# Twelve unused fp16 matmuls ahead of a wait in a patch-embedding, scan and feed-forward kernel

## The chip, the cores and the metric

The kernel runs on one core of one Trainium2 chip. The metric is the device time of one execution in microseconds, the median over several runs. "Before" took 1426.93 us (three runs, 1425.58 to 1428.28).

## The reference

Images and text tokens go through three layers. The image `x` (32, 3, 224, 224) is cut into 14 by 14 patches of 16 by 16 pixels, each patch is layer-normalised, multiplied by a 768 by 256 matrix and normalised again; the 77 text tokens are appended, which makes 273 tokens of 256 features for each of the 32 images. Then comes a recurrent layer on every second token, and a gated feed-forward layer on all of them:

```python
h = tok_ref(x, W, bias, ln1_g, ln1_b, ln2_g, ln2_b)          # patches: layernorm, matmul, layernorm
h = concatenate([h, txt], axis=1)                            # 196 + 77 tokens
# attention layer: x_sub = rmsnorm(layernorm(h))[:, ::2]; x_proj, gate = split(x_sub @ w_in.T + b_in)
#   state = tanh(state * A + x_t * Bm);  y_t = state @ sum(Cm) + Dv * x_t     for each step t
#   out = (y * silu(gate)) @ w_out.T + b_out, each row repeated for two tokens
h = h + attn_ref(layernorm(h), w_in, b_in, A, Bm, Cm, Dv, w_out, b_out, g_norm)
h = h + ffn_ref(layernorm(h), w_gate, w_up, w_down)          # silu(gate) * up, then down
```

## The kernel before, in words

The 273 tokens are handled in 20 groups of 14 (the last has 7): groups 0 to 13 are one row of image patches each, 14 to 19 are text. The groups go through a pipeline, and iteration i of the program works on several of them at once: it normalises the pixels of group i+1 (the part called "ahead"), turns and embeds group i and projects it ("pre"), runs the recurrence of group i-1 ("scan"), finishes the recurrent layer and does the feed-forward layer of group i-2 up to its product ("post"), and does the down projection and the store of group i-3 ("down"). Iterations 0 to 2 fill the pipeline, iterations 3 to 12 are a loop with all parts, 13 is the last with image work, then come the text iterations and a tail.

Inside an iteration the order of work on each engine is written out by hand as 56 slots. Slot n holds step n of the scan: VectorE multiplies the state by A into one of four PSUM banks (`grow`, line 771), TensorE adds the input by one fp16 matmul (`drive`, line 1218), ScalarE takes the tanh (`squash`, line 976). Every eighth slot TensorE also reads out y with 16 matmuls (`read_step`, line 1228). All other parts are hung into slots by the table `PLANS` (lines 65 to 113). Each engine executes its list strictly in order, with semaphore waits in it.

What lies around the change, in image iterations, on TensorE:

- `shrink` (lines 1400 and 1401), the down projection of group i-3, in slots 1 to 7.
- `turn` (line 1273), eight groups of transposes of the normalised pixels of group i, in slots 7 to 14, into the banks P[0] and P[1] by turns. ScalarE copies each group out into `xT` (`xT_copy`, line 993), and counts `xT_done`. `turn(6)` is the last but one and the last in P[0]; its copy brings `xT_done` to g*8+7.
- `attend` (lines 1326 to 1341), slots 15 and 16: the output projection of the recurrent layer of group i-2. It waits for `z_done`, then for `xT_done` at g*8+7 (the bank P[0] is free), writes the bias into P[0] (line 1335), and adds the products of `zT` and `out_w` (line 1338).
- `embed` (line 1288), slots 17 to 28, `average` (line 1247), slots 19 and 21, `turn_fx` (line 1357), slot 32, the feed-forward matmuls `ffn` (lines 1385 and 1386), slots 34 to 52, `turn_xa` (line 1305) and `project` (line 1321), slots 35 to 48.

What `attend` waits for is a chain outside TensorE. After the last read-out ScalarE copies y out of PSUM (line 982), SyncE sends it to DRAM and back in another layout (lines 651 and 657), and GpSimd adds the skip term and multiplies by the gate (`gating`, lines 1121 and 1125), which counts `z_done`. Behind `attend` come the residual sum on VectorE (line 867), the normalisation and the feed-forward layer.

`fx_hi` is the fp16 part of the transposed, normalised activations, a tile of 128 by 2 by 448; ScalarE writes it at slot 31 (line 1050), and only `ffn` reads it. 

Of the kernel before, what the change touches and what calls it, by code (L numbers as in the profile page):

```python
# [37 lines left out]
KF = CH * PATCH * PATCH // 128  # L38
RAWP = CH * B
BIASP = 96  # L40
XA_AFTER, X_AFTER, GATE_AFTER = 1, 2, 4
X_SCALE, B_SCALE = 16.0, 64.0
U_SCALE = X_SCALE * B_SCALE
# [131 lines left out]
def build(nc, x, txt, W, tok_bias, ln1_g, ln1_b, ln2_g, ln2_b, w_in, b_in, A, Bm, Cm, Dv, w_out, b_out,  # L175
# [8 lines left out]
    with ctx:  # L184
        def sb(name, shape, dt=FP32):
            return ctx.enter_context(nc.sbuf_tensor(name, shape, dt))

        def sem(name):
            return ctx.enter_context(nc.semaphore(name))
# [18 lines left out]

        bias_one = sb("bias_one", [BIASP, PT], BF16)
        bias_row = sb("bias_row", [BIASP, D], BF16)  # L210
        h = sb("h", [128, RING, CW])
# [35 lines left out]
        fx_hi, fx_lo = (fx_split[:, n * DB * TOK:(n + 1) * DB * TOK].bitcast(FP16)  # L247
                        .rearrange("p (j t) -> p j t", j=DB) for n in range(2))
# [13 lines left out]
        P = [ctx.enter_context(nc.psum_tensor(f"P{n}", [128, 512], FP32)) for n in range(2)]  # L262
# [192 lines left out]
        def setup_tensor(pe):  # L455
            pe.wait_ge(s_w, 48)
            for f in range(KF):
                mm = pe.matmul(Y[0:PT, 0:D], b1[:, f:f + 1].to_broadcast([128, PT]), w_st[:, f, :],
                               start=(f == 0), stop=(f == KF - 1))
            mm.then_inc(s_bias, 1)  # L460
            pe.wait_ge(s_cst, 16)
            tensor_body(pe, -1, general=False, **AHEAD)
            pe.wait_ge(s_wts, 48)
            for n, (blocks, _, _) in enumerate(turns):
                if n == NU:
                    pe.wait_ge(s_row, 1)
                for k, src in enumerate(blocks):
                    mm = pe.transpose(turn_of(n)[:, k * 128:k * 128 + 128], src, ident)
                mm.then_inc(s_tr, 1)
# [83 lines left out]
        xT_done = sem("xT_done")  # L553
# [651 lines left out]
        def tensor_body(pe, i, image, ahead, pre, scan, post, down, steps, general):  # L1205
            r, g, s, q, d = i + 1, i, i - 1, i - 2, i - 3
# [102 lines left out]
            def project(part, k):  # L1309
# [13 lines left out]
                if k == DB - 1:  # L1323
                    mm.then_inc(proj_ps, 1)

            def attend(k):

                pe.wait_ge(z_done, q + 1)

                if pre and image:  # L1330
                    pe.wait_ge(xT_done, g * 8 + 7)
                elif down:
                    pe.wait_ge(out_done, d * 2 + 1)
                if k == 0:
                    pe.matmul(P[0][0:PT, 0:2 * D], bias_one[:, :], bias_row[:, :].unsqueeze(1).to_broadcast([BIASP, 2, D]),
                              start=True, stop=False, skip_group_check=True)
                for j in range(DB):
                    mm = pe.matmul(P[0][0:PT, k * D:k * D + D], zT[:, j, k * PT:k * PT + PT], out_w[:, j, :],
                                   start=False, stop=(j == DB - 1), skip_group_check=True)
                if k == 1:  # L1340
                    mm.then_inc(attn_ps, 1)
# [63 lines left out]
            for slot in range(SLOTS):  # L1405
# [22 lines left out]
                if post:  # L1428
                    for k in parts_at(plan, "attend", slot):
                        attend(k)  # L1430
# [55 lines left out]
        with nc.Block() as block:  # L1486
# [29 lines left out]
            @block.tensor  # L1516
            def _(pe):
                setup_tensor(pe)
                tensor_body(pe, 0, general=False, **HEAD[0])
                pe.wait_ge(s_bst, 1)  # L1520
                pe.wait_ge(s_read, 1)
                pe.wait_ge(s_brow, 9)
                pe.wait_ge(s_flag, 1)


                flag = pe.value_load(large_flag[:, :], min_val=0, max_val=1)
                with pe.If(flag > 0):
                    bodies(pe, tensor_body, general=True)
                with pe.Else():
                    bodies(pe, tensor_body, general=False)  # L1530
# [30 lines left out]
```

## Time and profile before

| | |
|---|---|
| median of three runs | 1426.93 us (1425.58 to 1428.28) |
| profiled execution | 1428.12 us |
| its span, first to last instruction | 1426.3 us |
| TensorE busy | 1224.9 us, 86% |
| VectorE busy | 1085.5 us, 76% |
| ScalarE busy | 1001.3 us, 70% |
| GpSimd busy | 434.4 us, 30% |
| mean granted TensorE clock | 0.943 of full speed |

The profiled execution's own time lies 1.8 us above its span, which is what stands around the first and the last instruction. Busy shares say which engine has most to do on average, and not what the end of an iteration waits for. The granted clock is the share of full speed that the throttle gave TensorE in a stretch: 1.00 is 2.4 GHz, 0.50 is 1.2 GHz, and a value between is a mixture of the two over the stretch.

### The profile page before, as it was taken

Reading aid. Unit: us, or ns where it says so; the run is one execution under the profiler, and the core shown is the slowest. Engines: PE = TensorE matmul, PEld = TensorE weight load, DVE = VectorE, ACT = ScalarE, POOL = GpSimd, SP = SyncE. Lnnn points to the kernel's source line nnn. Section 1 sums busy time; section 2 is a strip of 40 time slices with the busy share of each in tenths; the row PEclk is TensorE's granted clock in tenths of the full one; section 3 lists DMA queues with packets and bytes.
Section 4 is the critical chain, followed back from the end, with each engine's and each line's share of the span. In section 5 each row is a group of like instructions: output and inputs, shape, how many; then the busy total and the mean of one; then the engine's idle time right before and its main releaser. Section 6 shows DMA issues by size and latency. Waiting matters only on the chain.

```text
span 1426.3 us, 25870 instructions
## 1 busy us (share of the span) xinstructions
PE 1224.9 (86%) x7137; PEld 662.5 (46%) x7137; DVE 1085.5 (76%) x2412; ACT 1001.3 (70%) x1955; POOL 434.4 (30%) x437
## 2 busy tenths in 40 slices
PE   2658898989898989898989889899999999998976
PEld 2434445445454444454545445454444444434434
DVE  4549787778787878787778777877888888887833
ACT  2437686767777677768685858586888787787732
POOL 7404042424242423333232333331311321321220
PEclk8769899999999999999899989999999999999987
DMA  6230414140404050505040414130323222322210
GB/s 183 56 75 28 104 31 112 28 115 26 116 26 115 17 123 6 132 6 126 16 120 22 116 26 104 38 81 23 92 67 94 78 77 76 80 77 58 75 36 15
DMA packets 154671, 99.60 MB, mean 70 GB/s; under 512 B 129057, under 2 KB 143265, under 8 KB 153281
## 3 DMA queue, kind: packets, MB, share of 16 engines
q1 hardware_dynamic: 151120, 97.58, 26.9%
q10 hardware_dynamic: 3504, 1.46, 0.5%
q8 instruction: 23, 0.38, 0.1%
q14 instruction: 24, 0.19, 0.0%
HBM read 58.39 MB, written 40.60 MB: 69 GB/s over the span
## 4 chain that ended last, share of the span: by engine, by line
PE 36%; issue 22%; DMA 10%; ACT 9%; POOL 9%; DVE 8%; SPq 5%; POOLq 0%; DVEq 0%; ACTq 0%
PE Y L1228 6%; PE U L1218 6%; DMA y_scr<-y_fx 6%; PE P L1385 5%; PE P L1288 5%; PE P L1386 5%; DVE U L771 3%; PE P L1321 3%; DMA yT<-y_scr 3%; ACT h L976 3%; ACT rawn L987 2%; SPq L651 2%; DVE act L891 1%; POOL yT L1121 1%; POOL zT L1125 1%
## 5 line engine op out<-in xcount | busy, mean ns | idle before, releaser
L771 DVE TENSOR_TENSOR U<-h,a_col 128x512 f32<-128x512 f32 x1096 | 704.5, 689 | 147.7 <-ACT h L976 146.7
L976 ACT ACTIVATE h<-U 128x512 f32<-128x512 f32 x1096 | 608.1, 603 | 240.8 <-PE U L1218 239.1
L1218 PE MATMUL U<-x_diag,b_st 128*128 128x512 f16 x1096 | 370.2, 388 | 63.0 <-DVE U L771 45.1
L1228 PE MATMUL Y<-h,read_st 128*32 128x512 f32 x2192 | 271.0, 613 | 0.7 <-ACT h L976 0.7
L1218 PEld LDWEIGHTS U<-x_diag,b_st 128*128 128x128 f16 x1096 | 105.1, 100 | 220.8 <-DVE U L771 146.0
L1160 POOL TENSOR_TENSOR xT_act<-act,xT_act 128x448 f16<-128x448 f32 x114 | 117.5, 1040 | 195.1 <-ACT xT_act L1060 194.1
L1288 PE MATMUL P<-tok_w,xT_act 128*112 128x256 f32 x672 | 169.7, 391 | 2.3 <-ACT xT_act L993 2.3
L1288 PEld LDWEIGHTS P<-tok_w,xT_act 128*112 128x112 f32 x672 | 120.2, 182 | 54.0 <-issue 21.2
L1400 PE MATMUL P<-down_w,xT_act 128*112 128x256 bf16 x480 | 118.5, 282 | 6.9 <-POOL xT_act L1160 4.6
L1228 PEld LDWEIGHTS Y<-h,read_st 128*32 128x32 f32 x2192 | 58.2, 111 | 138.4 <-issue 114.9
L1401 PE MATMUL P<-down_w,xT_act 128*112 128x256 bf16 x480 | 117.4, 279 | 0.0
L891 DVE SCALAR_TENSOR_TENSOR act<-fsg,P 128x448 f32<-128x448 f32 x118 | 72.6, 615 | 52.5 <-PE P L1386 51.9
L1121 POOL TENSOR_TENSOR yT<-yT,gate_in 128x448 f32<-128x448 f32 x20 | 22.7, 1134 | 260.9 <-DMA yT<-y_scr 260.9
L993 ACT ACTIVATE xT_act<-P 128x384 f32<-128x384 f32 x112 | 83.2, 804 | 15.1 <-PE P L1273 13.2
L1385 PE MATMUL P<-fx_split,gate_w 128*128 128x448 f16 x228 | 81.7, 358 | 10.8 <-DVE fx_split L896 10.1
L1385 PE MATMUL P<-fx_split,up_w 128*128 128x448 f16 x236 | 86.4, 366 | 4.6 <-DVE act L891 4.6
L778 DVE BATCH_NORM_STATS2 raw_st<-raw 96x6 f32<-96x256 f32 x196 | 70.1, 410 | 24.8 <-DMA raw<-in_x 24.8
L1386 PE MATMUL P<-fx_split,up_w 128*128 128x448 f16 x236 | 86.3, 366 | 0.0
L1056 ACT ACTIVATE fsg<-P 128x448 f32<-128x448 f32 x114 | 62.4, 547 | 33.2 <-PE P L1386 30.4
L1386 PE MATMUL P<-fx_split,gate_w 128*128 128x448 f16 x228 | 81.8, 359 | 0.0
L1321 PE MATMUL P<-xaT,in_w 128*128 128x224 f32 x320 | 76.0, 369 | 6.0 <-ACT xf L1026 4.9
L1110 POOL TENSOR_TENSOR res_s<-res_s,half_th 112x4 f32<-112x4 f32 x20 | 20.6, 1028 | 189.8 <-DVE res_s L881 189.8
(152 smaller groups left out, 1517.3 us busy)
## 6 DMA issues: line engine op xcount, KB each, us to landing
raw<-in_x SPq DMA_DIRECT2D x42, 448.0 KB, 6.1
gate_scr<-gate_o SPq DMA_DIRECT2D x20, 448.0 KB, 2.5
gate_in<-gate_scr SPq DMA_DIRECT2D x20, 448.0 KB, 7.7
tok_scr<-tok SPq DMA_DIRECT2D x19, 448.0 KB, 3.3
res<-tok_scr SPq DMA_DIRECT2D x19, 448.0 KB, 3.7
out<-res SPq DMA_DIRECT2D x76, 112.0 KB, 2.3
x_diag<-scan_scr SPq DMA_DIRECT2D x312, 16.0 KB
x_diag<-scan_scr SPq DMA_DIRECT2D x304, 12.0 KB
```

Of the source, the lines that this page charges most:

```text
L771: dve.tensor_tensor(U[bank_of(slot)][:, :].rearrange("p (l b) -> p l b", b=B), h[:, (slot - CHUNKS) % RING, :].rearrange("p (l b) -> p l b ...
L891: dve.scalar_tensor_tensor(act[:, k, :], fsg[:, k % 2, :], ACT_SCALE * DEQUANT, up_bank(k, scan)[:, 0:4 * PT], ALU.mult, ALU.mult).then_in ...
L976: sc.activation(h[:, slot % RING, :], U[bank_of(slot)][:, :], ACT.Tanh, scale=1.0 / U_SCALE).then_inc(squashed, 1)
L1160: gp.tensor_tensor(act_lo[:, k, :], act[:, k, :], act_hi[:, k, :], ALU.subtract).then_inc(act_lo_done, 1)
L1218: pe.matmul(U[bank_of(slot)][:, :], b_st[:, c, :], x_diag[:, c, :, t * B:t * B + B], start=False, stop=True, skip_group_check=True).then_i ...
L1228: mm = pe.matmul(Y[c4 * 32:c4 * 32 + 32, :], read_st[:, t, half, :], h[:, (t * CHUNKS + half * RG + c4) % RING, :], start=(t == 0 and half ...
L1288: mm = pe.matmul(P[1 - k // 2][0:PT, (k % 2) * D:(k % 2) * D + D], xT[:, f, k // 2, (k % 2) * PT:(k % 2) * PT + PT], tok_w[:, f, :], start ...
L1321: mm = pe.matmul(P[1][:, k * TOK:k * TOK + TOK], in_w[:, j, e0:e0 + 128], xaT[:, j, :], start=(j == 0), stop=(j == DB - 1))
L1385: pe.matmul(bank, half, fx_hi[:, j, :], start=(j == 0), stop=False)
L1386: mm = pe.matmul(bank, half, fx_lo[:, j, :], start=False, stop=(j == DB - 1))
L1400: pe.matmul(bank, act_hi[:, f, k * PT:k * PT + PT], half, start=(f == 0), stop=False)
L1401: mm = pe.matmul(bank, act_lo[:, f, k * PT:k * PT + PT], half, start=False, stop=(f == HB - 1))
```

## The change

A constant and a function are added, and `attend` calls the function once per iteration, at its first part, if the iteration has both a "pre" part and image work (iterations 2 to 13, since `attend` itself is only in iterations from 2 on). It waits for `xT_done` at g*8+7 first and then issues twelve fp16 matmuls of 448 columns into P[0]. Stationary and moving operand are both taken from `fx_hi`. All have start=True, nobody reads their result, and the bias matmul of `attend` overwrites the bank. The wait for `z_done` comes after them, and the old wait for `xT_done` stays where it was.

```diff
+FILL = 12
...
+            def keep_busy():
+                idle = fx_hi[:, 0, :]
+                for _ in range(FILL):
+                    pe.matmul(P[0][:, 0:448], idle[:, 0:128], idle[:, :], start=True, stop=True)
+
             def attend(k):
+                if k == 0 and pre and image:
+                    pe.wait_ge(xT_done, g * 8 + 7)
+                    keep_busy()
 
                 pe.wait_ge(z_done, q + 1)
```

## Rows read from the trace of the kernel before

**Rows 1.** The page: span with TensorE's share, and its granted clock in 40 slices.

```profile
span 1426.3 us, 25870 instructions
...
PEclk8769899999999999999899989999999999999987
```

**Rows 2.** Waits of TensorE: line waited for, us in total, times, longest.

```profile
PE U L1218 <- DVE U L771: 45.1, 86, 2.9
PE P L1335 <- POOL zT L1125: 30.1, 10, 3.1
```

**Rows 3.** Eight us behind each attend: PE, PEld, DVE, ACT, POOL busy, PEclk, DMA, GB/s.

```profile
167.06:175.06 8.00, 8.00 (x46) 4.90 (x47) 7.50 (x30) 3.96 (x9) 0.00 (x0) 1.00 0.07 12
237.69:245.69 8.00, 8.00 (x37) 4.58 (x38) 4.57 (x21) 2.28 (x4) 0.00 (x0) 0.80 0.36 91
311.13:319.13 8.00, 8.00 (x33) 4.37 (x33) 4.06 (x20) 2.28 (x4) 0.00 (x0) 0.69 0.34 83
384.14:392.14 8.00, 8.00 (x36) 4.54 (x37) 4.58 (x20) 2.28 (x4) 0.00 (x0) 0.79 0.34 84
456.52:464.52 8.00, 8.00 (x37) 4.63 (x38) 5.00 (x22) 2.28 (x4) 0.00 (x0) 0.82 0.35 84
529.89:537.89 8.00, 8.00 (x34) 4.37 (x34) 4.12 (x19) 2.28 (x4) 0.00 (x0) 0.71 0.35 84
602.74:610.74 8.00, 8.00 (x36) 4.55 (x37) 4.76 (x21) 2.28 (x4) 0.00 (x0) 0.79 0.35 83
675.20:683.20 8.00, 8.00 (x29) 4.72 (x33) 4.05 (x20) 2.28 (x4) 0.00 (x0) 0.62 0.34 83
749.60:757.60 8.00, 8.00 (x36) 4.58 (x37) 4.70 (x21) 2.28 (x4) 0.00 (x0) 0.79 0.35 83
821.99:829.99 8.00, 8.00 (x29) 4.70 (x33) 3.92 (x19) 2.28 (x4) 0.00 (x0) 0.62 0.35 83
896.44:904.44 8.00, 8.00 (x37) 4.59 (x37) 4.94 (x22) 2.28 (x4) 0.00 (x0) 0.79 0.33 83
967.29:975.29 8.00, 8.00 (x44) 4.85 (x45) 7.14 (x17) 4.07 (x9) 0.70 (x1) 1.00 0.11 21
```

**Rows 4.** Same columns, from 20 to 32 us behind three of the attends.

```profile
257.69:269.69 12.00, 9.57 (x49) 3.92 (x48) 10.67 (x25) 7.61 (x16) 4.88 (x7) 0.86 0.01 2
...
404.14:416.14 12.00, 9.28 (x56) 4.34 (x55) 10.58 (x25) 8.66 (x18) 4.99 (x7) 1.00 0.00 0
...
695.20:707.20 12.00, 9.79 (x52) 4.62 (x50) 10.05 (x25) 8.22 (x18) 5.00 (x7) 0.86 0.00 0
```

**Rows 5.** Same columns: the three us ahead of three attends.

```profile
308.13:311.13 3.00, 0.10 (x1) 0.01 (x1) 3.00 (x8) 2.02 (x5) 2.27 (x2) 0.68 0.50 146
...
526.89:529.89 3.00, 0.00 (x1) 0.01 (x1) 3.00 (x8) 1.89 (x4) 2.27 (x2) 0.63 0.50 147
599.74:602.74 3.00, 0.07 (x1) 0.01 (x1) 3.00 (x8) 1.99 (x5) 2.27 (x2) 1.00 0.50 146
```

**Rows 6.** Same columns: the 3.5 us ahead of one such stretch.

```profile
523.39:526.89 3.50, 2.77 (x22) 1.65 (x18) 3.50 (x10) 3.38 (x7) 0.00 (x0) 1.00 0.29 67
```

**Rows 7.** Timeline of TensorE around two attends: start, us, instruction, idle before it.

```profile
526.48 0.38 PE L1218 MATMUL U<-x_diag,b_st 128*128 128x512 f16 x1
529.89 0.67 PE L1335 MATMUL P<-bias_row,bias_one 96*112 96x512 bf16 x1 [3.02 <-POOL zT L1125]
...
967.29 0.39 PE L1335 MATMUL P<-bias_row,bias_one 96*112 96x512 bf16 x1 [0.15 <-ACT xT_act L993]
```

**Rows 8.** Timeline of TensorE: fp16 matmuls of 448 columns, at either clock.

```profile
264.16 0.35 PE L1386 MATMUL P<-fx_split,gate_w 128*128 128x448 f16 x1
264.35 0.35 PE L1385 MATMUL P<-fx_split,gate_w 128*128 128x448 f16 x1
...
703.21 0.58 PE L1386 MATMUL P<-fx_split,gate_w 128*128 128x448 f16 x1
703.58 0.58 PE L1385 MATMUL P<-fx_split,gate_w 128*128 128x448 f16 x1
```

**Rows 9.** Same stretch to one product: TensorE from attend to the first average, two iterations.

```profile
167.06:174.51 7.45, 7.45 (x41) 4.44 (x42) 7.10 (x26) 3.94 (x8) 0.00 (x0) 1.00 0.07 13
529.89:539.62 9.73, 9.73 (x41) 5.78 (x42) 5.76 (x23) 2.28 (x4) 0.00 (x0) 0.76 0.29 69
```

## The prediction

> **What bounds the kernel now.** I read the page first, then the waits of TensorE, then the granted clock stretch by stretch. The page gives a span of 1426.3 us and a clock that is rarely at full in a whole slice [rows 1]. The waits tell what can make a busy engine stop for long: ten times `attend` (line 1335) stands for the gated y from GpSimd, 30.1 us in all, 3.0 each; the larger sum, 45.1 us for VectorE's `grow`, is spread over 86 short waits [rows 2]. `attend` runs in twelve image iterations; in the first (167.06) and the last (967.29) it finds its y ready, and waits 0.15 us at most, for the copy that frees the bank [rows 7]. In the ten others TensorE does nothing for 3 us [rows 5].
>
> The stall itself is set by the way of y through DRAM and GpSimd, and the change does not touch it. What it costs beyond itself shows in the eight us behind each attend, in which TensorE is busy without a break. There the clock is 1.00 behind the two attends without a stall and 0.62 to 0.82 behind the ten with one [rows 3]. So the clock falls to its lower level (1.2 GHz) during the stall or as it ends, ten times in ten, and comes back only after 3 to 6 us of dense work. A stretch of 8 us at clock c leaves 8 x (1 - c) us of full-speed work undone. For the ten that is 8 x (0.20 + 0.31 + 0.21 + 0.18 + 0.29 + 0.21 + 0.38 + 0.21 + 0.38 + 0.21) = 20.6 us.
>
> Is that time on the path that sets the end? Two readings say so. From attend to the first `average`, 41 matmuls, TensorE needs 7.45 us at full clock and 9.73 at 0.76: 9.73 x 0.76 = 7.4, so the whole difference is the clock [rows 9]. And the iteration lengths, which are the differences of the starts in [rows 3], add up. The one from 167.06 to 237.69 is 70.63 us long and ends with a stall like the others, but has full clock behind its attend. I take that as the length without loss. The next nine are 73.44, 73.01, 72.38, 73.37, 72.85, 72.46, 74.40, 72.39 and 74.45. Taking off 70.63 and the loss behind their own attend (1.60, 2.48, 1.68, 1.44, 2.32, 1.68, 3.04, 1.68, 3.04) leaves 1.21, -0.10, 0.07, 1.30, -0.10, 0.15, 0.73, 0.08 and 0.78. Five are zero: **the loss passes into the iteration one for one.** The other four have a second fall. From 20 to 32 us behind attend TensorE's work is thin (9.3 to 9.8 busy of 12), and there the clock is 0.86 in five iterations (those from 237.69, 456.52, 675.20, 821.99 and 896.44) and 1.00 in the rest [rows 4]. This late fall costs (1.21 + 1.30 + 0.73 + 0.78) / 4 = 1.0 us each time.
>
> **The change, part by part.**
>
> *The fill in a stall.* TensorE comes to the place 3.0 us before y is ready, its last drive ending at 526.86 and attend beginning at 529.89 [rows 7]. The first new wait, for the seventh copy out of P[0], is met about then: where y is no hindrance, it costs 0.15 us [rows 7]. Twelve matmuls of 448 fp16 columns start 0.19 us apart at full clock and 0.37 apart at the lower one [rows 8]. So they take 12 x 0.19 = 2.3 us of the 3.0 and end about 0.6 us before y: no delay, their cover is the wait for GpSimd. At the lower clock they take 12 x 0.37 = 4.4 us and come out 1.5 us after y. Their weight loads lie beside the matmuls, as those of line 1385 do. Nothing else is moved. Queued behind them on TensorE are the two halves of attend and the next drive, and for these VectorE and ScalarE wait, as they do today.
>
> *What it gives.* If it holds the clock at 1.00 through every stall, the whole 20.6 us go. If it holds it nowhere, nothing goes. I take all ten as held but for part of two. In the stalls before 311.13 and 529.89 the clock fell early: 0.68 and 0.63 over three us is a lower clock for 1.9 and 2.2 us of them, so it fell 1.1 and 0.8 us into the stall [rows 5]. By then the fill has run for a third of its length. I put 1.5 us in for such early falls (one stall in ten at the full 1.5 us of delay; ends 0 and 15).
>
> *The fill without a stall.* In the iterations at 167.06 and 967.29 there is nothing to hide it. TensorE is busy throughout the 8 us behind [rows 3] and, as [rows 9] show, any loss there passes on. This costs 2 x 2.3 = **4.5 us**, at the least 0 if slack further on takes it up.
>
> *The late fall.* It is not the fill's work, but the fill decides what it meets. Whether the clock falls in the thin stretch depends on how the iteration lies against the chip's own judging of it, and the record shows it at 26.5 to 27.2 us behind attends with 1.6 as with 3.0 us lost before; it is no narrow target. Now it hits five of ten. With iterations shorter and nearly alike, hits may repeat in all or in none. The ends are 0 and 12 falls. Their price is 0.73 to 1.30 us each by the rows above; should the clock stay low for twice as long, as behind 675.20 (loss 3.04, [rows 3]), up to 3.0. I take nine at 1.2, 10.8 in place of today's 5.0: **5.8 us lost**. I lean high because a stretch that is busy for about three quarters and that drops the clock in half the iterations is likelier to be met when the iteration's length settles.
>
> *The sum.* -20.6 + 4.5 + 1.5 + 5.8 = **-8.8 us**. Against the profiled execution's own 1428.1 us that is 1419.3 us. That execution lies 1.2 us over the median of the runs shown (1426.93), so a median could as well come out at 1418.
>
> **The rivals.**
>
> *Clock held, and few late falls.* Same mechanism with the late falls at 0 to 5: -20.6 + 4.5 = -16.1, and up to 5.0 more. 1407 to 1412 us. Against it: the thin stretch remains as it is. Chance 0.07.
>
> *The clock falls in spite of the fill.* What stands ahead of the stall is a mixture: 22 matmuls in 3.5 us, most of them the transposes of `turn`, TensorE busy for 2.77 us [rows 6]. If these count for little with the throttle, the fall is under way when the fill begins. Then the fill runs at the lower clock, attend comes 1.5 us late, but the fill has been dense and the clock is back sooner. Per stall that is 1.5 + about 0.3 of remaining loss against 2.06 today, a gain of 0.26; ten of those and the 4.5 us give +1.9, so 1430 us, and 1427 to 1433 with the number of such stalls. For it: two early falls out of ten. Against it: the clock was 1.00 all through the stretch of [rows 6], and in eight of ten stalls it held for over 1.1 us of pure idling. Chance 0.18. The Trainium skill speaks for this rival ("TensorE: Matmul & The Clock Gate", Part 4, on PE-mode transposes): a transpose does not count as TensorE being busy in the way that a matmul does. By that rule alone the time would be the 1430 us of this rival; the trace shows transposes and matmuls only mixed, so it neither agrees nor disagrees.
>
> *Slower: the thin stretch goes low for long, in every iteration.* Place: 20 to 32 us behind attend, where today the second fall sits. If without the loss behind attend the iteration comes to lie so that the clock falls at the start of the thin stretch and too little work follows to bring it back at once, the price is that of the long low stretch, 3.0 us instead of 1.0. Ten of those are 30 for today's 5: -20.6 + 4.5 + 1.5 + 25 = +10.4, 1438 us. It decides from a mean of (5.0 + 14.6) / 10 = 2.0 us per iteration on. For it: low stretches of both lengths occur. Against it: all five late falls were short. Chance 0.08, at 1430 to 1438.
>
> *The gain is hidden elsewhere.* If, with TensorE faster, the chain of GpSimd and the DMAs sets the iteration, half the gain goes: -10.3 + 4.5 + 3 = about -3, 1425 us. Against it is the iteration of 70.63 us, which had all of the gain. Chance 0.07.
>
> **How the numbers follow.** The forecast has the remaining 0.60, with 1414 to 1424 as its own range (late falls from 5 to 12, at 1.0 to 1.3 us, early ones 0 to 3 us). The predicted time is its 1419.3. For 8 times in 10 the range runs from 1410 to 1429: it takes in the forecast, the hidden gain, the upper part of the first rival and the lower half of the second. It leaves out the third rival, the upper half of the second and the lowest end. About 0.2% (2.9 us) is what a measurement of this kernel can tell from no change. Faster than 1424.1: 0.56 of the forecast, 0.07 of the first rival and 0.02 of the last, 0.65. Slower than 1429.8: 0.10 of the second and 0.07 of the third, 0.17. Between: 0.18.
>
> **What would show it.** Right: in the profile after, the eight us behind the ten attends at 0.95 to 1.00; twelve matmuls 0.19 us apart before each, with 0.5 to 0.7 us of idling between the last and line 1335; the wait for GpSimd down from 30.1 to about 6 us; iterations of 71.7 to 72 us where a late fall is in them and 70.6 where none is; the clock 0.86 from 20 to 32 us behind most attends; the first attend 2.3 us later than 167.06. Wrong: matmuls of the fill 0.37 us apart and line 1335 up to 1.5 us late (the second rival), a clock under 0.80 from 20 to 32 us (the third), or full clocks and iterations still above 72.5 us (the last).

## The result, and the profile after

The changed kernel takes 1418.83 us (median of six, 1416.83 to 1422.02), the kernel before 1427.61 us beside it (six, 1423.47 to 1431.68). The ratio is 0.9938, with a 95% interval of 0.9915 to 0.9962: 8.8 us or 0.6% faster. The forecast was 1419.3 us and 8.8 us less.

The page after, the same two parts as [rows 1]:

```profile
span 1418.6 us, 26168 instructions
...
PEclk8769899999999999999999999999999999999988
```

The waits of TensorE after, to be held against [rows 2] (lines behind the change have moved; attend's bias matmul is line 1344, its products line 1347, `grow` 772):

```profile
PE U L1219 <- DVE U L772: 46.7, 91, 3.9
...
PE P L1344 <- POOL zT L1126: 5.0, 10, 0.8
```

TensorE now waits 0.5 us for the gated y instead of 3.0. That alone is no gain, since y comes no sooner; the timeline of TensorE shows what stands in its place:

```profile
524.05 0.38 PE L1219 MATMUL U<-x_diag,b_st 128*128 128x512 f16 x1
524.50 2.44 PE L1330 MATMUL P<-fx_split 128*128 128x448 f16 x12
527.21 0.42 PE L1344 MATMUL P<-bias_row,bias_one 96*112 96x512 bf16 x1 [0.27 <-POOL zT L1126]
```

From the start of the last drive to line 1344 it is 3.16 us here and 3.41 in [rows 7], so the fill fits into the stall, as the sum had it. What it is worth stands in the eight us behind attend, columns as in [rows 3]. Three rows of twelve; all twelve show 1.00:

```profile
169.04:177.04 8.00, 8.00 (x47) 4.90 (x46) 5.93 (x28) 2.31 (x5) 0.00 (x0) 1.00 0.02 3
240.87:248.87 8.00, 8.00 (x45) 4.93 (x46) 5.99 (x28) 2.28 (x4) 0.00 (x0) 1.00 0.34 91
...
670.72:678.72 8.00, 8.00 (x45) 4.93 (x46) 6.21 (x29) 2.28 (x4) 0.00 (x0) 1.00 0.36 83
```

In the same eight us the profile counts 45 matmuls of TensorE, and 29 in [rows 3] at 675.20. From 20 to 32 us behind attend (columns as in [rows 4]) the clock is now 0.86 in all twelve image iterations. Two of the rows:

```profile
260.87:272.87 12.00, 9.57 (x52) 3.96 (x50) 9.85 (x26) 8.29 (x18) 3.39 (x6) 0.86 0.00 1
...
547.21:559.21 12.00, 9.56 (x51) 3.86 (x49) 9.67 (x25) 8.10 (x17) 3.40 (x6) 0.86 0.00 0
```

The two kernels cut at the first attend and at the attend of iteration 14, first before, then after:

```profile
167.06:1035.37 868.31, 776.26 (x4564) 428.97 (x4565) 684.96 (x1573) 636.74 (x1242) 289.69 (x304) 0.96 0.27 67
1035.37:1426.30 390.93, 345.39 (x2073) 172.67 (x2071) 298.54 (x558) 282.41 (x563) 81.01 (x82) 0.96 0.25 67
```

```profile
169.04:1025.27 856.23, 790.39 (x4697) 432.02 (x4696) 683.35 (x1570) 634.42 (x1238) 290.28 (x304) 0.98 0.27 67
1025.27:1418.60 393.33, 346.80 (x2073) 174.22 (x2071) 298.70 (x558) 282.87 (x563) 81.09 (x82) 0.96 0.25 66
```

The twelve image iterations are 12.1 us shorter, the start is 2.0 longer (iteration 2 has a fill there; how much of this is the fill's comes below), and the rest 2.4 longer, in which nothing was changed: 7.7 us less in the span.

### The profile page after: what moved, and what is told of

The parts are those of the page before. It is cut to its first block, busy times and chain, and to the rows that moved or that the text cites. A ratio compares the mean times of both kernels' runs of the same rounds, so it can differ in the third digit from the quotient of the medians.

```text
span 1418.6 us, 26168 instructions
## 1 busy us (share of the span) xinstructions
PE 1243.2 (88%) x7281; PEld 668.6 (47%) x7281; DVE 1086.0 (77%) x2412; ACT 1001.2 (71%) x1955; POOL 435.1 (31%) x437
## 4 chain that ended last, share of the span: by engine, by line
PE 45%; issue 14%; DVE 10%; DMA 10%; ACT 9%; POOL 6%; SPq 4%; DVEq 0%; POOLq 0%; ACTq 0%
PE Y L1229 9%; PE P L1289 8%; PE U L1219 7%; PE P L1394 6%; DMA y_scr<-y_fx 6%; PE P L1395 6%; DVE U L772 4%; PE P L1322 3%; DMA yT<-y_scr 3%; ACT h L977 3%; ACT rawn L988 2%; SPq L652 2%; PE P L1347 1%; POOL yT L1122 1%; POOL zT L1126 1%
## 5 line engine op out<-in xcount | busy, mean ns | idle before, releaser
L1229 PE MATMUL Y<-h,read_st 128*32 128x512 f32 x2192 | 266.7, 604 | 0.7 <-ACT h L977 0.7
L1394 PE MATMUL P<-fx_split,gate_w 128*128 128x448 f16 x228 | 85.9, 377 | 11.1 <-DVE fx_split L897 10.4
L1394 PE MATMUL P<-fx_split,up_w 128*128 128x448 f16 x236 | 90.1, 382 | 4.7 <-DVE act L892 4.7
L779 DVE BATCH_NORM_STATS2 raw_st<-raw 96x6 f32<-96x256 f32 x196 | 70.1, 410 | 24.4 <-DMA raw<-in_x 24.4
L1395 PE MATMUL P<-fx_split,up_w 128*128 128x448 f16 x236 | 88.7, 376 | 0.0
L1395 PE MATMUL P<-fx_split,gate_w 128*128 128x448 f16 x228 | 86.4, 379 | 0.0
L1274 PE MATMUL P<-cst,rawn 96*128 96x96 f32 x392 | 57.7, 273 | 22.5 <-ACT xT_act L994 10.1
```

The costliest lines, as they stand in the source:

```text
L1229: mm = pe.matmul(Y[c4 * 32:c4 * 32 + 32, :], read_st[:, t, half, :], h[:, (t * CHUNKS + half * RG + c4) % RING, :], start=(t == 0 and half ...
L1394: pe.matmul(bank, half, fx_hi[:, j, :], start=(j == 0), stop=False)
L1395: mm = pe.matmul(bank, half, fx_lo[:, j, :], start=False, stop=(j == DB - 1))
```

## The experiments

Ten kernels were run, each timed against the kernel before. They are called e1 to e10, in the order in which they stand here. Each quoted text is what was expected before the run; a code cut shows only the lines that matter.

**e1: the wait without the matmuls.**

```diff
-FILL = 12
+FILL = 0
```

> FILL = 0: the early wait for the seventh copy stays, the twelve matmuls go. Theory (the matmuls hold the clock, the wait is free): the time of before within 0.2%, 1425 to 1431 us, TensorE idle 3.0 us ahead of ten attends, granted clock 0.62 to 0.82 in the eight us behind them. Rival (the gain comes from the order of the waits or from the layout of the program): about 1419 us, as with the change.

Measured: 1425.47 us against 1425.75, ratio 0.9997 (0.9982 to 1.0013). Eight us behind two of its attends:

```profile
239.27:247.27 8.00, 8.00 (x37) 4.57 (x38) 4.47 (x21) 2.28 (x4) 0.00 (x0) 0.79 0.36 93
...
605.10:613.10 8.00, 8.00 (x29) 4.70 (x33) 4.08 (x20) 2.28 (x4) 0.00 (x0) 0.62 0.33 83
```

The falls are back and the gain is gone. The wait costs nothing, and the gain is the matmuls' alone.

**e2: the fill in the loop only.**

```diff
-                if k == 0 and pre and image:
+                if k == 0 and pre and image and not isinstance(i, int):
```

> The fill only in iterations 3 to 12, not in the two without a stall (2 and 13). Theory that the fill there costs its full length on the path: 4 us less than the change, about 1415 us. Rival (the late fall of the clock repeats once per iteration and its place in the iteration takes back what is given): within 1 us of the change, 1418 to 1420 us.

Measured: 1414.22 us, ratio 0.9911 (0.9888 to 0.9934). That is 4.6 us less than the change by the medians and 0.0027 less by the ratios, 3.9 us; the two were timed beside different runs of before, and their intervals overlap. The pair e5 and e6 below repeats the comparison within one set of runs and gives 3.6 us. So the fill costs most of its length where no stall covers it.

This trace shows one thing more. TensorE came to the attend of iteration 2 three us earlier than in the kernel before (its last drive started at 163.39 instead of 166.54), and so had a stall of 2.8 us there, with no fill in it. The timeline, the eight us behind it, and the eight us behind the next attend, whose stall was filled:

```profile
166.58 0.42 PE L1344 MATMUL P<-bias_row,bias_one 96*112 96x512 bf16 x1 [2.81 <-POOL zT L1126]
```

```profile
166.58:174.58 8.00, 8.00 (x36) 4.47 (x37) 5.34 (x23) 2.28 (x4) 0.00 (x0) 0.79 0.08 16
239.08:247.08 8.00, 8.00 (x45) 4.93 (x46) 5.32 (x22) 2.28 (x4) 0.00 (x0) 1.00 0.38 92
```

The one stall without a fill lost the clock, and the ten with one kept it, in one execution. Whether iteration 2 has a stall thus differs from trace to trace.

**e3: a fill in the thin stretch, slot 34.**

```diff
+FILL, LATE = 12, 3
...
-            def keep_busy():
+            def keep_busy(n=FILL):
...
                     pe.wait_ge(fxT_done, (q + 1) * 4)
+                    if pre and image:
+                        keep_busy(LATE)
                     pe.wait_ge(fx_lo_done, (q + 1) * 2)
```

> The change and three more such matmuls (0.19 us each) in slot 34, between the waits for fxT_done and fx_lo_done ahead of the first feed-forward matmul, in the same twelve iterations; they lie in 0.67 us of idling. Theory (a clock fall in the thin stretch costs 1.0 to 1.1 us in each of twelve iterations and more work there prevents it): granted clock 1.00 from 20 to 32 us behind every attend, iterations of 70.6 us, 12 us less than the change, about 1407 us. Rival (the fall comes anyway, or shifts elsewhere): within 2 us of the change, iterations still 71.7 us.

Measured: 1415.91 us, ratio 0.9922 (0.9900 to 0.9944), against 0.9938 for the change: no difference that these intervals show. The late fall (the second fall of the prediction, in the thin stretch from 20 to 32 us behind attend) was still in ten of twelve iterations. The timeline of TensorE in one of them:

```profile
548.84 0.39 PE L1219 MATMUL U<-x_diag,b_st 128*128 128x512 f16 x1 [0.90 <-DVE U L772]
549.44 0.61 PE L1219 MATMUL U<-x_diag,b_st 128*128 128x512 f16 x1 [0.21 <-DVE U L772]
549.84 1.33 PE L1330 MATMUL P<-fx_split 128*128 128x448 f16 x3
```

The drive at 549.44 already takes 0.61 us where the one before it took 0.39: the clock fell ahead of the added matmuls, which then run at the lower level. They came too late to matter.

**e4: transposes for matmuls.**

```diff
-                for _ in range(FILL):
-                    pe.matmul(P[0][:, 0:448], idle[:, 0:128], idle[:, :], start=True, stop=True)
+                for _ in range(21):
+                    pe.transpose(P[0][:, 0:128], ident, ident)
```

> The twelve matmuls are replaced by 21 transposes of a 128 by 128 fp32 block into the same bank, about as long (0.11 us each, 2.3 us). Theory that any stream through TensorE holds the clock: as with the change, clock 1.00 behind all attends, 1417 to 1421 us. Rival (transposes do not count as work for the clock): clock 0.62 to 0.82 behind the attends with a stall, and 2.2 us paid in each of two iterations without one, 1429 to 1434 us.

Measured: 1416.91 us, ratio 0.9935 (0.9913 to 0.9957). The fill on the timeline of TensorE, and the eight us behind that attend:

```profile
523.63 2.51 PE L1330 MATMUL P<-cst 128*128 128x128 f32 x21
526.45 0.42 PE L1344 MATMUL P<-bias_row,bias_one 96*112 96x512 bf16 x1 [0.30 <-POOL zT L1126]
```

```profile
526.45:534.45 8.00, 8.00 (x45) 4.93 (x46) 6.09 (x28) 2.28 (x4) 0.00 (x0) 1.00 0.33 83
```

All twelve attends have 1.00. These transposes of fp32 blocks hold the clock as well as the fp16 matmuls do, and the main ground of the second rival is gone.

**e5: two fills in the thin stretch.** As e3, and ahead of the transposes in slot 32, into P[1]. A second early wait, for `tok_small`, is added there:

```diff
             def turn_fx(j):
+                if j == 0 and pre and image:
+                    pe.wait_ge(tok_small, g * 16 + 2)
+                    keep_busy(LATE, P[1][:, 0:448])
                 pe.wait_ge(fx_done, (q + 1) * 4)
```

> The change with the three matmuls of e3 in slot 34 and three more in slot 32, ahead of the transposes of turn_fx, into P[1], in 0.66 us of idling. In e3 the clock fell 23.7 us behind attend, before its added matmuls began. Theory (the fall is brought on by the thin work of the three us ahead of it, so work there prevents it): clock 1.00 from 20 to 32 us in most iterations, 70.6 us each, 8 to 12 us less than the change, 1406 to 1411 us. Rival (late falls cost 1 us per iteration wherever one puts work): 1415 to 1419 us.

Measured: 1403.93 us, ratio 0.9853 (0.9836 to 0.9869), better than expected. The ratio is 0.0085 under that of the change, 12.1 us. Between the two profiles it is 13.0 us up to iteration 14 (attend at 1012.30 instead of 1025.27) and 3.5 us in the rest, where nothing was changed. The clock is 1.00 from 20 to 32 us behind every attend, and the ten iterations that end in a stall take 70.35 to 70.78 us, the 70.63 of the one undisturbed iteration of before. A row, and the timeline around slot 34:

```profile
541.17:553.17 12.00, 10.41 (x63) 4.58 (x61) 10.26 (x27) 9.36 (x20) 3.39 (x6) 1.00 0.00 0
```

```profile
541.49 0.73 PE L1330 MATMUL P<-fx_split 128*128 128x448 f16 x3
542.32 0.99 PE L1369 MATMUL P<-cst,y_fx 112*128 112x112 f32 x8
544.20 0.39 PE L1219 MATMUL U<-x_diag,b_st 128*128 128x512 f16 x1 [0.90 <-DVE U L772]
544.80 0.39 PE L1219 MATMUL U<-x_diag,b_st 128*128 128x512 f16 x1 [0.21 <-DVE U L772]
545.02 0.73 PE L1330 MATMUL P<-fx_split 128*128 128x448 f16 x3
```

What the fill of slot 32 adds shows in the stretch from 21.0 to 24.3 us behind attend. In the change the clock falls at its end; here it holds. First the change, then e5:

```profile
548.20:551.50 3.30, 1.76 (x10) 0.96 (x10) 3.12 (x10) 2.80 (x6) 0.00 (x0) 1.00 0.00 0
...
542.17:545.47 3.30, 2.10 (x14) 1.22 (x13) 3.12 (x10) 2.79 (x6) 0.00 (x0) 1.00 0.00 0
```

The last of the twelve iterations was not free of falls: it had one some 51 us behind its attend, outside the stretch (the clock is 0.69 from 994.50 to 1000.00).

**e6: the same, with the fill of the stall in the loop only** (e5 with the edit of e2).

> As e5, and the twelve matmuls of the stall only in iterations 3 to 12. Theory: the 4.4 us that e2 saved come on top, 1402 to 1407 us. Rival (the saving of e2 was a matter of where the falls lay): as e5.

Measured: 1400.31 us, ratio 0.9830 (0.9808 to 0.9851). This is the best version: 1.7% faster than before, and 1.1% by the ratios under the change. It came out 3.6 us under e5, and all four of its runs (1397.56 to 1402.63) lie under all four of e5 (1403.13 to 1404.85).

**e7: the late fills without the fill of the stall** (e5 with FILL = 0).

> The two late fills of e5 without the twelve matmuls of the stall (the early wait stays). Theory of two separate costs, 20.6 us for the falls in the stalls and 1.0 us for each late one: only the five or six late falls of before go, 4 to 6 us less than before, 1420 to 1423 us, clock 0.62 to 0.82 behind the ten attends. Rival (work in the thin stretch alone gives most of the gain): under 1418 us.

Measured: 1422.48 us against 1425.23, ratio 0.9989 (0.9973 to 1.0005). By its time alone this can't be told from before. The clocks are plain: 0.62 to 0.82 behind the ten attends with a stall, and 1.00 from 20 to 32 us behind every one. So the late falls can be removed while those in the stalls stay, and the stalls are the larger cost. The lengths of the iterations say it more sharply than the time. The nine from 237.20 on take 71.75 to 73.57 us; less the loss behind their own attend, 8 x (1 - c) as in the prediction, they take 70.3 to 70.9, on average 70.6, and those of e5 take 70.5 with no loss at all. One of the attends with the largest loss, whose iteration takes 73.57 us:

```profile
453.77:461.77 8.00, 8.00 (x29) 4.71 (x33) 4.30 (x20) 2.28 (x4) 0.00 (x0) 0.62 0.32 88
```

**e8: half the fill.**

```diff
-FILL = 12
+FILL = 6
```

> FILL = 6: 1.1 us of matmuls at the head of each 3.0 us stall, and half the cost in the two iterations without one. Theory that what counts is how little of the stall is left idle: the clock falls in about half of the stalls, 10 us of the 20.6 come back and 2.2 us are paid, 1417 to 1424 us. Rival A (any work in the stall holds the clock): 1414 to 1417 us, clocks as with twelve. Rival B (only an unbroken stream does): 1427 to 1430 us.

Measured: 1415.23 us, ratio 0.9931 (0.9914 to 0.9949), not to be told from twelve. One of its stalls on the timeline of TensorE, and eight us behind two attends:

```profile
380.20 1.31 PE L1330 MATMUL P<-fx_split 128*128 128x448 f16 x6
383.28 0.66 PE L1344 MATMUL P<-bias_row,bias_one 96*112 96x512 bf16 x1 [1.76 <-POOL zT L1126]
```

```profile
383.28:391.28 8.00, 8.00 (x36) 4.54 (x37) 4.84 (x21) 2.28 (x4) 0.00 (x0) 0.79 0.36 84
455.60:463.60 8.00, 8.00 (x45) 4.94 (x46) 6.20 (x29) 2.28 (x4) 0.00 (x0) 1.00 0.33 83
```

The clock fell in four of eleven stalls. An iteration that lost 1.7 us behind its attend had no late fall; six of the other eight had one. The four falls in stalls were offset by six late falls in place of twelve. Of the seven stalls that held the clock, six had 1.14 to 1.61 us idle behind the matmuls and one 1.80; the four that lost it had 1.74 to 1.89. The time falls into the range of rival A, and the clocks lie between it and the theory (half of the stalls).

**e9: slot 32 alone** (e6 without the three matmuls in slot 34).

> As e6 without the three matmuls in slot 34; those in slot 32 stay. Theory (the thin work ahead of 23.7 us behind attend decides, the added work of slot 34 lies behind it and is of use only once iterations have no fall): the late falls are gone in most iterations, 1400 to 1404 us. Rival (both are needed, the fall moves behind the filled place): falls in half or more of the iterations or all, 1405 to 1413 us.

Measured: 1412.96 us, ratio 0.9908 (0.9887 to 0.9929), the rival; e2, without the fill in slot 32, had 0.9911, so alone this fill gives nothing that can be told. The same holds for the early wait for `tok_small`, which is in this kernel too. The late fall was in ten of twelve iterations, from 24.2 to 25.4 us behind attend. The timeline of TensorE:

```profile
332.03 0.39 PE L1219 MATMUL U<-x_diag,b_st 128*128 128x512 f16 x1 [0.21 <-DVE U L772]
333.09 0.56 PE L1397 MATMUL P<-fx_split,gate_w 128*128 128x448 f16 x1 [0.67 <-DVE fx_split L897]
333.44 0.58 PE L1398 MATMUL P<-fx_split,gate_w 128*128 128x448 f16 x1
```

The last drive still runs at full clock, the first feed-forward matmul no longer. In the change the fall begins 23.8 to 24.4 us behind attend. One of them, in which the clock is 0.75 over a microsecond, so that it fell in its middle (24.35 us behind attend):

```profile
551.06:552.06 1.00, 0.33 (x2) 0.13 (x2) 1.00 (x3) 0.27 (x1) 0.00 (x0) 0.75 0.00 0
```

In e3 it begins at 23.5 to 23.7, just ahead of the added matmuls. So either fill alone shifts the fall by a few tenths of a microsecond, by 1.6 at most, and only both together remove it. Why both are needed is open.

**e10: twenty-four in the stall** (e2 with FILL = 24).

> As e2 (fill in iterations 3 to 12 only) with 24 matmuls in place of 12: 4.5 us of matmuls in a stall of 3.0 us. Theory (TensorE at attend is on the path, the stall covers 3.0 us and no more): attend comes 1.5 us later in ten iterations, 15 us more than e2, about 1429 us. Rival (slack further on takes up part): 1418 to 1424 us.

Measured: 1426.13 us against 1425.62, ratio 0.9997 (0.9980 to 1.0015), 11.9 us more than e2 (12.3 by the ratios; the two were not timed side by side). The timeline of TensorE shows the overrun: no wait for y is left ahead of line 1344.

```profile
380.81 4.71 PE L1330 MATMUL P<-fx_split 128*128 128x448 f16 x24
385.36 0.38 PE L1344 MATMUL P<-bias_row,bias_one 96*112 96x512 bf16 x1
```

Of its six iterations without a late fall that have a loop fill at their end, five take 72.2 to 72.3 us, 1.7 more than the 70.5 of e5 (the sixth takes 73.1). Over ten iterations that is 17, less the late falls that it lacks (six, against ten in e2, at 1.07 us: 4.3). It also lacks the fall behind the first attend of e2, another 1.7 us. That makes 11.0, and from the first attend to that of iteration 14 the two profiles take 865.3 and 854.2 us, 11.1 more. The overrun passes on in full, and an expected 15 came out as 12 because fewer falls came.

## Why the prediction was right

**The stall (-20.6 us).** Confirmed as worked out. The clock behind the ten attends is 1.00 where it was 0.62 to 0.82, and e1 and e7 show the old clocks as soon as the twelve matmuls are taken away, with the wait still there in both. Over all traces, the 31 stalls of 2.7 us and more without a fill (before, e1, e2, e7) had 0.62 to 0.83 behind them, and the 70 attends of the loop with twelve matmuls or 21 transposes ahead (the change, e2 to e6, e9) all had 1.00. That the loss passes into the iteration one for one was read off the iteration lengths of before; e5, with neither kind of fall, has nine iterations in a row at 70.35 to 70.73 us, and e7, with the falls in the stalls alone, comes down to the same length once each loss is taken off.

**The fill without a stall (+4.5).** Somewhat less. The first attend comes 2.0 us later. The iteration that ends in the last of the twelve attends takes 71.02 us, where it took 70.85 with a loss of 1.68 behind its attend; this is 1.85 us for the fill. Together 3.8, and e5 against e6 gives 3.6 us. But the 2.0 is one pair of traces: with nothing filled there, the first attend came at 165.79 to 167.86 in seven traces (on average 166.7), and with twelve matmuls or 21 transposes at 167.40 to 169.04 in four (168.0). On average the fill costs 1.3 us there. The prediction took iteration 2 to have no stall, as in its trace; e2 and e6 show one of 2.8 and of 1.6 us, which can cover a part.

**Early falls (+1.5).** None came. The price was taken from two stalls in which the clock fell within 1.1 us [rows 5]; none of the ten stalls of the change lost its clock.

**The late fall (+5.8).** The prediction read the clock as 1.00 in all but five iterations of before [rows 4]. The last of the twelve, from 967.29, had a late fall as well, which is six of twelve:

```profile
987.29:999.29 12.00, 10.14 (x54) 4.15 (x53) 9.01 (x24) 8.60 (x19) 1.51 (x3) 0.86 0.00 0
```

It changes nothing in the sum, as that iteration has its fall before and after. The side was right and the count low: nine were taken, of the first eleven iterations five had one before and all eleven have one after. The price was a little high, 1.2 us for the 1.07 measured: the nine loop iterations from 240.87 on take 71.45 to 72.06 us, on average 71.7, less 70.63. With the 70.5 of e5 as the length without loss it is 1.16, nearly the price taken. Six more falls at 1.07 are 6.4 us. So -20.6 + 3.8 + 6.4 = -10.4 up to iteration 14, and the trace has 12.1 - 2.0 = 10.1. What the sum did not contain is the rest of the program, 390.9 us before and 393.3 after. It holds no edit, and in e4 it took 386.5 us (its row, from the attend of iteration 14 to the end), at a clock of 0.98 (over all twelve traces 386.5 to 394.1):

```profile
1026.10:1412.60 386.50, 339.52 (x2073) 168.75 (x2071) 298.66 (x558) 282.28 (x563) 81.02 (x82) 0.98 0.25 67
```

That part varies by several us with where the clock falls in it, and a sum over the image iterations can miss as much. That the forecast and the measured time agree to 0.5 us is in part luck: the terms left out and the terms put too high nearly cancel.

**The rivals.** Few late falls (1407 to 1412 us) did not occur by itself; brought about in e5 by two more fills, it came to 1403.9 us. The clock falling in spite of the fill is refuted for this fill, and e4 takes away its main reason. The Trainium skill's rule behind that rival ("TensorE: Matmul & The Clock Gate", Part 4: a transpose does not count as TensorE being busy in the way that a matmul does) is not borne out by e4, where 21 fp32 transposes in each stall kept the granted clock at 1.00 (the page speaks of TensorE's transpose mode; the trace records these as matmuls of 128x128 fp32 and does not show the mode). The long low stretch did not come: the clock from 20 to 32 us was never under 0.86. Nothing else hid the gain.

Why the late fall came in every iteration of the change is explained only in part. The iterations after are alike to within 0.6 us, so if one meets the fall, the next lies in nearly the same way. That a different length would have escaped it was not shown by a run that changed the length alone; e10, with iterations of 72.2 to 73.5 us, had it in six of twelve.

## What to carry to other kernels

Where TensorE stands for something that can't be hurried, read the granted clock behind the wait as well as the wait: here a wait of 3.0 us cost another 2.1. Unused matmuls can win that back if they are shorter than the stall, go into a bank that is overwritten anyway and are left out of iterations that have no stall. Look at more than one trace for which those are. Then look for the next place where the clock falls: in this kernel a stretch without any long wait took 1.07 us of every iteration, and it had to be filled at two places at once, since one fill alone only shifted the fall a little.

## What was not expected of the hardware

- Without a wait of a microsecond the clock fell too: in the thin stretch the longest pause of TensorE is 0.90 us, it is busy 9.6 of 12 us and 1.76 of the 3.3 us ahead of a fall, yet the fall came in twelve of twelve iterations of the change.
- Six matmuls (1.31 us) at the head of a 3.0 us stall, with 1.1 to 1.9 us idle behind them, held the clock in seven of eleven stalls.
- Three matmuls (0.57 us by their spacing) at either of two places 3.5 us apart left the late fall in ten of twelve iterations; with three at both places none was left from 20 to 32 us behind attend.
